# One comparison per block of edges, with the edge tiles innermost, in the counting stage of a graph network kernel

## The reference

```
x = ln(x + SAGE(x))        # two mean aggregations over x[src] by dst
x = ln(x + MESSAGE(x))     # an MLP on each edge, summed by dst
x = ln(x + GCN(x))         # sum of x[src] by dst, weighted by degrees
x = ln(x + GIN(x))         # sum of x[src] by dst
```

## Time and profile before

| what | us |
|---|---|
| median of 3 runs | 1868.16 |
| the three runs | 1865.35, 1868.16, 1868.62 |
| span of the profiled execution (no other time of it is listed) | 1867.8 |
| stretch of the counting stage in it | 38.1 to 300.6 |

### The profile page before, as it was taken

The page is one execution under the profiler, slowest core; times in us unless marked ns, Lnnn a source line. Parts: engine busy times, 40 slices in busy tenths (PEclk is TensorE's granted clock), DMA queues, the critical chain, the costliest instruction groups (busy, mean ns, idle before and its releaser), DMA issues.

```text
span 1867.8 us, 33710 instructions
## 1 busy us (share of the span) xinstructions
PE 1584.5 (85%) x10288; PEld 1027.3 (55%) x10289; DVE 758.1 (41%) x2774; ACT 708.7 (38%) x1406; POOL 763.3 (41%) x798
## 2 busy tenths in 40 slices
PE   2777777998997788889999998999999899563995
PEld 1444445444455566666666766667666676331444
DVE  7988895113223322233324324333332333376004
ACT  4666664002001344445445445444544444302001
POOL 4000000000000677777777777777777777100000
PEclk9999997999998899999999999999999999785998
DMA  1000000000002433333333333333333333000001
GB/s 56 0 0 0 0 0 3 1 1 14 26 0 75 125 83 81 82 85 83 83 80 87 83 80 86 81 84 80 86 83 81 82 83 84 13 5 3 0 0 35
DMA packets 158369, 93.99 MB, mean 50 GB/s; under 512 B 120529, under 2 KB 143824, under 8 KB 158296
## 3 DMA queue, kind: packets, MB, share of 16 engines
q0 software_dynamic: 25088, 51.43, 10.6%
q1 hardware_dynamic: 133208, 41.60, 9.2%
HBM read 86.44 MB, written 6.52 MB: 50 GB/s over the span
## 4 chain that ended last, share of the span: by engine, by line
PE 39%; POOL 8%; issue 6%; DVE 6%; DMA 6%; ACT 2%; SPq 1%; DVEq 1%; POOLq 0%; ACTq 0%
POOL arena L669 8%; PE ps L915 6%; PE ps L907 6%; PE ps L900 6%; PE ps L788 6%; PE ps L888 4%; DMA arena<-x_w1a,idx 4%; PE ps L896 3%; PE ps L964 3%; PE ps L923 2%; DVE arena L1505 1%; DMA arena<-in_edge_attr 1%; DVE stats L1495 1%; ACT arena L1257 1%; ACT arena L1255 1%
## 5 line engine op out<-in xcount | busy, mean ns | idle before, releaser
L669 POOL DMA_INDIRECT arena<-x_w1a,idx x784 | 744.4, 949 | 830.0 <-issue 803.7
L788 PE MATMUL ps<-adj,arena 128*128 (+2 forms) x1575 | 316.2, 363 | 14.9 <-DVE arena L1470 8.1
L788 PEld LDWEIGHTS ps<-adj,arena 128*128 128x128 bf16 x1575 | 146.1, 99 | 179.5 <-issue 29.3
L915 PEld LDWEIGHTS ps<-arena 128*24 128x24 f32 x1568 | 145.9, 103 | 157.3 <-issue 100.9
L1651 DVE TENSOR_TENSOR arena<-ps,bias_b 128x512 f32<-128x512 f32 x196 | 135.6, 692 | 215.1 <-PE ps L907 215.1
L722 PE MATMUL ps<-arena 128*128 128x300 bf16 x784 | 165.1, 296 | 63.1 <-DVE arena L1457 63.1
L907 PE MATMUL ps<-w_c,arena 128*128 128x128 f32 x1568 | 211.8, 279 | 0.0
L915 PE MATMUL ps<-arena 128*24 128x128 f32 x1568 | 207.5, 275 | 2.4 <-ACT arena L1223 2.2
L1111 ACT ACTIVATE adj<-ps 128x300 f32 x392 | 166.9, 450 | 97.4 <-PE ps L727 91.9
L1646 DVE TENSOR_TENSOR arena<-win_i,drel 128x96 f32<-128x96 f32 x196 | 50.6, 258 | 375.0 <-PE ps L915 369.6
L900 PE MATMUL ps<-arena 88*128 88x512 f32 x392 | 201.9, 596 | 0.3 <-ACT arena L1213 0.3
(11 more groups left out here) (164 smaller groups left out, 1374.9 us busy)
## 6 DMA issues: line engine op xcount, KB each, us to landing
arena<-in_edge_attr SPq DMA_DIRECT2D x196, 128.0 KB
arena<-x_w1a,idx POOLq DMA_INDIRECT x784
arena<-x_w1b SPq DMA_DIRECT2D x196, 12.0 KB
x_spill<-arena SPq DMA_DIRECT2D x1, 1600.0 KB, 7.7
x_w1a<-arena SPq DMA_DIRECT2D x6, 256.0 KB, 2.3
x_w1b<-arena SPq DMA_DIRECT2D x6, 256.0 KB, 2.7
arena<-x_spill SPq DMA_DIRECT2D x6, 256.0 KB
out_x<-arena SPq DMA_DIRECT2D x3, 512.0 KB
```

Source lines behind the costliest of these rows:

```text
L669: pool.indirect_dma_start(out=z_e[v][:, j * D:(j + 1) * D], out_offset=None, in_=xa_d[:, :], in_offset=bass.IndirectOffsetOnAxis(ap=idx[:, ...
L788: last = pe.matmul(ps[:, u, 0:w], parts[q][:, k, :], adj[:, k, bass.ds(c0, w)], start=(k == 0 and q == 0), stop=(k == NT - 1 and q == 2))
L915: last = pe.matmul(ps[0:WIN, 1, 0:D], oh_e[v][:, j, :], msg[:, j * P:(j + 1) * P], start=(j == 0), stop=(j == J - 1))
```

## The change

`oh_dst` is laid out with the tile innermost, as `oh_src` already is: 300 values by 4 tiles, so the element (n, j) lies at 4 n + j. One comparison of 128 x 1200 elements fills it, of a ramp `iota_c` that now holds each value four times against the block's four columns of `comb`, repeated 300 times by a broadcast. For this `comb` becomes int16 (it was fp32, as the comparison with a column as scalar takes it). TensorE reads the moving operand of tile j with a step of four elements, 8 bytes. `iota_j` moves by 128 words to make room, and the memsets of `comb`'s unused end write an integer.

```
--- before.py
+++ after.py
@@ -124,15 +124,15 @@
         p_rel = raw_src.bitcast(F32)
 
         oh_dst = [arena[:, 600 * v:600 * v + J * NT * WIN_A // 2].bitcast(BF16)
-                  .rearrange("p (j n) -> p j n", j=J) for v in range(4)]
+                  .rearrange("p (n j) -> p n j", j=J) for v in range(4)]
         oh_src = [arena[:, 9024 + 256 * v:9280 + 256 * v].bitcast(BF16).rearrange("p (n j) -> p n j", j=J)
                   for v in range(4)]
-        comb = arena[:, 2912:2912 + NB * J].rearrange("p (s j) -> p s j", j=J)
+        comb = arena[:, 2912:2912 + NB * J // 2].bitcast(I16).rearrange("p (s j) -> p s j", j=J)
         lo_h = arena[:, 3696:3696 + NB * J // 2].bitcast(BF16).rearrange("p (s j) -> p s j", j=J)
         base_a = arena[0:1, 4088:4088 + 2 * NB].bitcast(I32)
         falls = arena[0:1, 2400:2400 + 2 * NB - 2]
-        iota_c = arena[:, 8000:8000 + NT * WIN_A // 2].bitcast(I16)
-        iota_j = arena[:, 8512:8512 + P * J // 2].bitcast(BF16).rearrange("p (n j) -> p n j", j=J)
+        iota_c = arena[:, 8000:8000 + J * NT * WIN_A // 2].bitcast(I16).rearrange("p (n j) -> p n j", j=J)
+        iota_j = arena[:, 8640:8640 + P * J // 2].bitcast(BF16).rearrange("p (n j) -> p n j", j=J)
 
         KE = R + WIN
 
@@ -617,7 +617,7 @@
                                      base=0, pattern=[[-1, P]], channel_multiplier=1))
             g.add(pool.affine_select(out=ident_h[:, :], in_=ident_h[:, :], compare_op=ALU.not_equal, fill=1.0,
                                      base=0, pattern=[[-1, P]], channel_multiplier=1))
-            g.add(pool.iota(iota_c, pattern=[[1, NT * WIN_A]], base=0, channel_multiplier=0))
+            g.add(pool.iota(iota_c, pattern=[[1, NT * WIN_A], [0, J]], base=0, channel_multiplier=0))
             g.add(pool.iota(win_i[:, :], pattern=[[1, WIN]], base=0, channel_multiplier=0,
                             allow_small_or_imprecise_dtypes=True))
             g.add(pool.memset(ones_h[:, :], 1.0))
@@ -719,7 +719,7 @@
                 if h == 0:
                     pe.wait_ge(oh_ready, 4 * i + v + 1)
                 for j in (2 * h, 2 * h + 1):
-                    last = pe.matmul(ps[:, q, 0:NT * WIN_A], oh_src[v][:, :, j], oh_dst[v][:, j, :],
+                    last = pe.matmul(ps[:, q, 0:NT * WIN_A], oh_src[v][:, :, j], oh_dst[v][:, :, j],
                                      start=(j == 2 * h), stop=False)
                 if h == 1:
                     last.then_inc(oh_used, 1)
@@ -1443,9 +1443,9 @@
             dve.memset(words(20, 22), 0)
             dve.wait_ge(prep_out, 8)
             dve.memset(src_idx[:, NB, :], 0)
-            for a in (comb, drel):
-                dve.memset(a[:, NB - 1, 0:DUP // P], -1.0)
-                dve.memset(a[0:DUP % P, NB - 1, DUP // P:DUP // P + 1], -1.0)
+            for a, none in ((comb, -1), (drel, -1.0)):
+                dve.memset(a[:, NB - 1, 0:DUP // P], none)
+                dve.memset(a[0:DUP % P, NB - 1, DUP // P:DUP // P + 1], none)
             phase_end(dve, 1)
 
 
@@ -1453,9 +1453,8 @@
                 s = unit_block(i, v)
                 dve.wait_ge(oh_used, 4 * i + v + 1)
                 dve.tensor_tensor(oh_src[v], iota_j, lo_h[:, bass.ds(s, 1), :].broadcast_to([P, P, J]), ALU.is_equal)
-                for j in range(J):
-                    last = dve.tensor_scalar(oh_dst[v][:, j, :], iota_c, comb[:, bass.ds(s, 1), j], None, ALU.is_equal)
-                last.then_inc(oh_ready, 1)
+                dve.tensor_tensor(oh_dst[v], iota_c, comb[:, bass.ds(s, 1), :].broadcast_to([P, NT * WIN_A, J]),
+                                  ALU.is_equal).then_inc(oh_ready, 1)
 
             with dve.Fori(0, GRP // 2) as i:
                 for v in range(4):
```

## The result

The changed kernel takes 1930.16 us (median of 4 runs, 1929.41 to 1930.88) against 1867.48 (4 runs): a ratio of 1.0327, 95% interval 1.0315 to 1.0339. Nothing like 1870 and outside the stated range; it is the rival with the halved stream, and worse than that by 13 us. Of all executions reported here one, of `j_twos`, ran in a slower state (2356 us at a granted clock of 0.65); it is left out of that run's median and ratio.

A forecast was written before the change was run, and what follows sets the result against it. The prediction took TensorE's units at ScalarE's pace plus TensorE's own queue gap as the bound, with VectorE hidden. First blocks -0.3, ramp +2.2 and TensorE 0 gave +1.9 us, so 1870 us; range 1861 to 1878.

The forecast's parts named there:

- the rival with the halved stream: TensorE's count matmuls: streaming with a step runs at half the rate, iteration 6.3 instead of 5.36 us, 1917; chance 0.08.
- What bounds the stage: Count stage: TensorE's units at ScalarE's pace plus 1.39 us of TensorE's own queue per iteration; VectorE hidden.
- VectorE's term: Count stage: the wide comparison takes 784 ns, 0.13 us less a block, 25 us over 196, costed at nothing.
- some 50: Sign for being right: VectorE's waits for TensorE in the count stage go from 25 to some 50 us.
- The first blocks: Start of the count stage: two uncovered blocks, each 0.13 us shorter, -0.3 us.
- GpSimd's ramp: Preparation: iota_c grows from 300 to 1200 elements and delays the memset that VectorE's first shift waits for, +2.2 us.
- TensorE: Count stage: 784 matmuls of 300 columns reading every fourth element cost nothing extra, 0 us.
- the sign that the prediction named for being wrong: In the profile: L722 matmuls over 330 ns, a comparison near 1.4 us, or a period under 5.1 us with matmuls unchanged.
- its threshold: Count stage: the half-rate rival decides once a unit passes ScalarE's 0.50 us, at 60 ns more a matmul.

The follow-up runs named there:

- j_twos: The change with two tiles innermost instead of four, so TensorE streams with a step of two; 1871.28 us against 1867.93 for the kernel before, ratio 1.0014.
- g_pairs: Kernel before with one 128x1200 comparison per block, one-hots still tile by tile, comb holding each value twice; 1866.66 us against 1865.75, ratio 1.0006.
- e_sweep2: Kernel before with count matmuls streaming 300 zeros in eight patterns (steps 1 to 5, rows of 2 or 4); 1882.24 us, one run.
- f_unroll: Kernel before with seven counting iterations written out on TensorE and ScalarE, next window starts read mid-iteration; 1846.07 us against 1865.75, ratio 0.9898.

## Why the prediction was wrong

- **What bounds the stage**: right. VectorE was hidden; the comparison alone gives 1.0006, with the loop written out it gives nothing either, and the time between iterations came down with VectorE untouched. Of the 1.39 us the branch and the read are 0.80; the rest, which I did not list, is register operations on the same queue.
- **VectorE's term**: right, 776 ns for 784, and its waits in g_pairs are 48.7 us for "some 50".
- **The first blocks**, -0.3 us: about half of it shows (in g_pairs TensorE's first matmul starts at 39.43 instead of 39.57). **GpSimd's ramp**, +2.2: measured 2.12 us for the ramp, 1.74 more than before, and all of it reached VectorE's first comparison (39.99 against 38.25). The place and the mechanism were right, the size 0.5 too high.
- **TensorE**, "I take 0": this is the step that failed, and with it the forecast. The step of four costs 0.250 us between matmuls instead of 0.127, 123 ns for each of 784, of which 58 us come through; the sign that the prediction named for being wrong, matmuls over 330 ns, is there with 444. I had the row that speaks for a price, 113 against 96 ns for a weight load with the same step, and set it aside by a reading of my own, that at half the clock both loads take 152 ns, "so the 17 ns belong to loading at full speed, which is another path". Beside it stood the rule of the Trainium skill, "SBUF — State Buffer", in its note on cachelines, whose two hits are short by half at the full clock. But for the stream the experiments show just such a price, one that is there at the full clock and gone at half of it: a fixed time per line, as long as four columns at 2.4 GHz and two at 1.2. That the weight load's 17 ns are the same line time is not shown. Its duration is no clean price either, for in the changed kernel the contiguous loads of the identity, 96 ns before, last as long as the stepped ones:

```profile
L727 PEld LDWEIGHTS ps<-adj,ident_h x392: 110/116/128, 41.4 to 359.5; 128*128 128x128 bf16 x196
```

- **The rival at half the rate** had the right mechanism for this step, though not the rule (half the rate at any step is refuted by step 2), and its threshold was nearly right (45 ns against 60). It gave 1917 for 1930, the ramp's 2 us included. An iteration was to take 6.3 us and takes 6.55 over the stage, which makes 12 of the 13. Two errors go against each other in it. The units take 5.34 us where 7 x 0.63 + 0.5 gives 4.9: the second stepped matmul holds the identity matmul 0.27 us, not 0.25, and the identity matmul itself then takes 0.15 to 0.19 where I had put 0.13. And the gap is 1.09 us, not 1.39, because TensorE's queue runs ahead of the slower matmuls: in the trace the branch starts 0.28 us before the last identity matmul (248.43 and 248.71), where before it started 0.02 ahead (204.01 and 204.03). Its chance of 0.08 was far too low for the nearest row on its side, and the range left it out.

## What to carry to other kernels

A layout in which the tiles are interleaved for the elementwise engine is paid for by the engine that picks them apart: count the 16-byte lines that TensorE's moving operand touches and allow 1.7 ns for each, so at the full clock two-byte elements are all but free at a step of two and pay from three on. If one wide comparison is wanted and the stream is to stay contiguous, double the small operand so that its innermost pair are neighbours, as in g_pairs. And before work is taken from the busiest engine, look at who waits for whom in the order of time: here it was hidden, and the 20 us that were to be had lay in the branch and the register work at the top of TensorE's loop. The read itself stays on the queue, and reading more at once saved nothing.

## What the runs showed of the hardware that was not expected

- TensorE's stream is limited to one 16-byte line in 1.7 ns at either level of its clock (table above): 0.250 us for 300 columns at a step of 4 elements at 2.4 GHz instead of 0.127, and next to no loss at 1.2 GHz (a pair takes 0.71 us for 0.69).
- Reading registers from memory scales with their number on TensorE's queue: 0.59 us for 8, 1.62 for 24, 2.13 for 32.
- A weight load's duration is not its own alone: the identity's loads took 96 ns before and 116 in the changed kernel, where nothing of theirs had changed. In e_sweep2 they took 113 ns behind step 4 and 96 behind all other patterns, step 5 too (medians of the trace). What sets it is open.
- That VectorE stood only 8 us in the stage of f_unroll didn't make it the bound: taking 25 us of its work away changed nothing.
- GpSimd wrote the same ramp of 1200 in 2.12 us ahead of the memset and 2.56 behind it, when VectorE was at work; 600 elements took 1.62. What sets these is open.
